# Turned tiles between the gate and the up product, and one layer norm's root on ScalarE, in a fused four-layer kernel

## The reference

```python
x = x + _layernorm(_L0_attn_ref(_layernorm(x), ...))   # state-space layer
x = x + _layernorm(_L0_ffn_ref(_layernorm(x), ...))    # 4-bit gated feed-forward
x = x + _layernorm(_L1_attn_ref(_layernorm(x), ...))   # attention over heads
x = x + _layernorm(_L1_ffn_ref(_layernorm(x), ...))    # mixture of experts
...
def _L0_ffn_ref(x, ...):
    gate = x2 @ Wg          # [1024, 512] @ [512, 1376]
    up = x2 @ Wu
    inter = gate * jax.nn.sigmoid(gate) * up
    out = (inter @ Wd).astype(jnp.float16)
...
def _layernorm(x, axis=-1, eps=1e-05):
    m = jnp.mean(x, axis=axis, keepdims=True)
    v = jnp.var(x, axis=axis, keepdims=True)
    return (x - m) / jnp.sqrt(v + eps)
```

## Time and profile before

| | |
|---|---|
| time, 3 runs | median 820.5 us (820.09 to 820.9) |
| profiled execution | 822.49 us, its span 820.6 us |
| TensorE busy | 691.6 us (84%) |
| VectorE busy | 690.7 us (84%) |
| ScalarE busy | 462.8 us (56%) |
| GpSimd busy | 488.0 us (59%) |
| granted TensorE clock, mean | 0.904 of full speed |

### The profile page before, as it was taken

The page is one execution under the profiler, slowest core; times in us unless marked ns, Lnnn a source line. Parts: engine busy times, 40 slices in busy tenths (PEclk is TensorE's granted clock), DMA queues, the critical chain, the costliest instruction groups (busy, mean ns, idle before and its releaser), DMA issues. The chain is left out here.

```text
span 820.6 us, 8369 instructions
## 1 busy us (share of the span) xinstructions
PE 691.6 (84%) x2770; PEld 326.2 (40%) x2770; DVE 690.7 (84%) x694; ACT 462.8 (56%) x783; POOL 488.0 (59%) x258
## 2 busy tenths in 40 slices
PE   7979899988685978465648879999999999999993
PEld 6623333322121323111112224444445447787882
DVE  6789899999999999999999999997364656585668
ACT  5477768777655774957554445675334447233321
POOL 2429989999999999999999920300002014340251
PEclk9999989999788998666857879999999999999997
DMA  7443122335404623633136129970040030000011
GB/s 252 95 135 103 67 101 94 125 128 198 161 4 151 208 79 139 180 128 109 46 103 215 42 78 241 244 219 5 1 153 1 1 103 0 1 1 1 0 52 51
DMA packets 42001, 82.39 MB, mean 100 GB/s; under 512 B 6743, under 2 KB 10240, under 8 KB 41704
## 3 DMA queue, kind: packets, MB, share of 16 engines
q1 hardware_dynamic: 41960, 81.87, 31.3%
HBM read 70.65 MB, written 11.21 MB: 100 GB/s over the span
## 5 line engine op out<-in xcount | busy, mean ns | idle before, releaser
L2211 POOL TENSOR_TENSOR dbu<-rep_du,bc 128x1024 f32<-128x1024 f32 x127 | 296.5, 2359 | 4.3 <-DMA rep_du<-rep_scratch 2.3
L1748 ACT ACTIVATE psum<-rep_dt,aneg 128x512 f32<-128x512 f32 x256 | 166.1, 682 | 116.7 <-DVE hc L1162 99.4
L1151 DVE TENSOR_TENSOR_SCAN psum<-psum,dbu 128x1024 f32<-128x1024 f32 x89 | 203.5, 2286 | 6.6 <-ACT psum L1748 5.0
L925 PE MATMUL psum<-hc,stk 128*32 128x512 f32 x512 | 85.4, 744 | 67.0 <-POOL hc L2220 50.0
L1162 DVE TENSOR_TENSOR hc<-psum,bc 128x1024 f32<-128x1024 f32 x89 | 109.0, 1224 | 3.1
L2220 POOL TENSOR_TENSOR hc<-hc,bc 128x1024 f32<-128x1024 f32 x39 | 91.8, 2354 | 6.0 <-DVE hc L1151 6.0
L1151 DVE TENSOR_TENSOR_SCAN hc<-psum,dbu 128x1024 f32<-128x1024 f32 x39 | 89.0, 2281 | 2.1 <-POOL dbu L2211 1.3
L680 PE MATMUL psum<-xf_hi,gu_hi 128*128 128x512 f16 x176 | 66.8, 379 | 1.3 <-DVE gu_lo L1209 0.7
L680 PE MATMUL psum<-xf_lo,gu_hi 128*128 128x512 f16 x176 | 66.7, 379 | 0.0
L680 PE MATMUL psum<-xf_hi,gu_lo 128*128 128x512 f16 x176 | 66.7, 379 | 0.0
L680 PE MATMUL psum<-xT,w_g 128*128 128x512 f32 x120 | 61.0, 658 | 2.6 <-ACT rep_du L1893 2.6
(11 more groups left out here) (268 smaller groups left out, 1450.9 us busy)
## 6 DMA issues: line engine op xcount, KB each, us to landing
rep_dt<-rep_scratch SPq DMA_DIRECT2D x60, 256.0 KB, 3.4
rep_du<-rep_scratch SPq DMA_DIRECT2D x60, 256.0 KB, 4.2
cw<-c_scratch SPq DMA_DIRECT2D x11, 768.0 KB, 10.5
qw<-qgu_in SPq DMA_DIRECT2D x11, 512.0 KB, 5.8
bc<-bc_scratch SPq DMA_DIRECT2D x16, 256.0 KB, 4.9
rep_scratch<-du_t SPq DMA_DIRECT2D x14, 256.0 KB, 2.0
rep_scratch<-dt_t SPq DMA_DIRECT2D x14, 256.0 KB, 2.3
qw<-qd_in SPq DMA_DIRECT2D x11, 256.0 KB, 7.1
```

The lines of the kernel that those rows point to most:

```text
L925: last = pe.matmul(y_rows(k), stk[:], hc[:, (i + k // 2) % HCS, k % 2, :], start=False, stop=(s == GN - 1))
L1151: dve.tensor_tensor_scan(h, a, dbu[:, i % DBS].rearrange("p e t -> p (e t)"), 0.0, ALU.mult, ALU.add)\
L1748: last = act.activation(psum[:, 2 * (i % 2) + e, :], rep_dt[:, cc % 2, k, :], ACT.Exp, scale=aneg[:, k, c, n:n + 1])
L2211: pool.tensor_tensor(dbu[:, i % DBS], rep_du[:, cc % 2, k:k + 2, :], bc[:, n, :].unsqueeze(1).broadcast_to([P, 2, L]), ALU.mult).then_inc( ...
```

## The change

1. In batch 1, at i = 4 (att) and i = 9 (moe), TensorE turns tiles 0 and 1 between g(i) and u(i), and tiles 2 and 3 between u(i) and down(i - 1); before, all four came behind down(i - 1).
2. To go with it, VectorE normalises all four tiles in the step before (i = 3 and i = 8), and takes the low halves of moe tiles 0 and 1 there too; ScalarE copies tiles 0 and 1 between the Silu and the cast of it_hi.
3. The statistics of ("out", 1) go from VectorE to ScalarE: a sum of each of four tiles between the weight casts ahead of step 0 (`sums_out`), four squares behind Silu(0), and behind Silu(1) a table load, root and shift (`own_root`). The bodies of `less_mean`, `squares` and `own_root` are those already used for batch 0's output.
4. The Silu table is asked for explicitly behind it_hi(1) and behind the roots at k = 5 and at i = 2, 6 and 8 of batch 1.

```diff
@@ -99,6 +99,7 @@
 
 
 TURN_FIRST = IC - NT
+TURN_BETWEEN = {4: "att", 9: "moe"}
 SSM_EARLY = 3
 OWN_PLACE = [item for items in SIDE.values() for item in items if item[0] == "dt"]
 ABS_AT = {2: 4, 3: 4, 7: 4}
@@ -136,13 +137,14 @@
         if i >= TURN_FIRST:
             items += [("tr", "ffn", 1, i - TURN_FIRST)]
     for i in range(IC):
-        items += [("g", 1, i), ("u", 1, i)]
-        if i == 4:
-            items += [("tr", "att", 0, t) for t in range(NT)]
+        items += [("g", 1, i)]
+        if i in TURN_BETWEEN:
+            items += [("tr", TURN_BETWEEN[i], 0, t) for t in range(2)]
+        items += [("u", 1, i)]
+        if i in TURN_BETWEEN:
+            items += [("tr", TURN_BETWEEN[i], 0, t) for t in range(2, NT)]
         if i == 5:
             items += [("qkv", 0)]
-        if i == 9:
-            items += [("tr", "moe", 0, t) for t in range(NT)]
     for b in range(NB):
         items += [("lt", b), ("routed", b, 0), ("logits", b)]
         items += [("routed", b, t) for t in range(1, NT)]
@@ -964,18 +966,15 @@
                             parts += halves(gu_hi[:, i, w], gu_lo[:, i, w], xf_hi[b][:, kk, :],
                                             xf_lo[b][:, kk, :])
                         product(item, parts).then_inc(work_ready, 1)
+                        if b == 1 and i in TURN_BETWEEN:
+                            for t in range(2 * j, 2 * j + 2):
+                                turn(TURN_BETWEEN[i], 0, t, xnc)
                     if i >= 1:
                         down(i - 1)
                     if b == 0 and i >= TURN_FIRST:
                         turn("ffn", 1, i - TURN_FIRST, obuf[1])
-                    if b == 1 and i == 4:
-                        for t in range(NT):
-                            turn("att", 0, t, xnc)
                     if b == 1 and i == 5:
                         qkv_part(0)
-                    if b == 1 and i == 9:
-                        for t in range(NT):
-                            turn("moe", 0, t, xnc)
                 down(IC - 1)
 
 
@@ -1219,8 +1218,8 @@
                     dve.tensor_tensor(xf_lo[b][:, :, cols], bank(item).rearrange("p (k t) -> p k t", k=KH),
                                       xf_hi[b][:, :, cols], ALU.subtract).then_inc(taken_sem(item), 1)
 
-            def low_moe(b):
-                for t in range(NT):
+            def low_moe(b, tiles=range(NT)):
+                for t in tiles:
                     item = ("tr", "moe", b, t)
                     cols = slice(t * P, (t + 1) * P)
                     dve.wait_ge(xmhi_done, NT * b + t + 1)
@@ -1466,18 +1465,10 @@
                     unpack(i + 3)
                 if i:
                     ffn_low(0, i)
-                if i == 1:
-                    for t in range(NT):
-                        wait_taken(dve, ("out", 1, t))
-                    stats(("out", 1), [obuf[1][:, t, :] for t in range(NT)])
                 if i == 5:
                     dve.wait_ge(out_done, NB * NT)
+                    dve.wait_ge(stats_ready, LN[("ffn", 1)])
                     stats(("ffn", 1), x_tiles(1))
-                if i == 2:
-                    inv_std(("out", 1), NT)
-                    n = LN[("out", 1)]
-                    dve.scalar_tensor_tensor(nmr1[:], mv[:, n, :, 0], -1.0, rstd[:, n, :], ALU.mult, ALU.mult)\
-                        .then_inc(nmr_ready, 1)
                 if i == 6:
                     inv_std(("ffn", 1), NT)
                     n = LN[("ffn", 1)]
@@ -1492,24 +1483,24 @@
 
             for i in range(IC):
                 ffn_times(1, i)
-                if i == 9:
-                    norm_tile("moe", 0, 2, xnc)
-                    norm_tile("moe", 0, 3, xnc)
                 ffn_low(1, i)
                 if i == 0:
                     dve.wait_ge(ld_att, 16 * 7)
                     dve.tensor_reduce(wqkv[:, :, 0:DH], wqraw[:], AX.X, ALU.add).then_inc(wq_done, 1)
                     dve.tensor_reduce(bqkv[:, 0:DH], bqraw[:], AX.X, ALU.add).then_inc(wq_done, 1)
-                if i < 8:
+                if i < 8 and i != 4:
                     between(0, i)
+                if i == 3:
+                    between(0, 4)
                 if i == 7:
                     between(0, 8)
                 if i == 8:
                     inv_std(("moe", 0), NT)
-                    norm_tile("moe", 0, 0, xnc)
-                    norm_tile("moe", 0, 1, xnc)
+                    for t in range(NT):
+                        norm_tile("moe", 0, t, xnc)
+                    low_moe(0, [0, 1])
                 if i == 9:
-                    low_moe(0)
+                    low_moe(0, [2, 3])
 
 
             def route(b):
@@ -2025,8 +2016,8 @@
                 act.copy(gu_hi[:, i, :], w[:, 0:2 * KH * P]).then_inc(whi_done, 1)
                 act.copy(d_hi[:, i, :], w[:, 2 * KH * P:]).then_inc(whi_done, 1)
 
-            def high_moe(b):
-                for t in range(NT):
+            def high_moe(b, tiles=range(NT)):
+                for t in tiles:
                     item = ("tr", "moe", b, t)
                     wait_work(act, item)
                     act.copy(xm_hi[b][:, :, t * P:(t + 1) * P], bank(item).rearrange("p (k t) -> p k t", k=KH))\
@@ -2052,6 +2043,10 @@
                     act.wait_ge(ffn_used, k - 1)
                 act.copy(it_hi[:, k % 2, :], it[:, k % 2, :]).then_inc(ithi_done, 1)
 
+            def sums_out(t):
+                wait_taken(act, ("out", 1, t))
+                link(act.activation(spare[:], obuf[1][:, t, :], ACT.Identity, accum_out=asum[:, t:t + 1]))
+
             def take16(b):
 
                 act.wait_ge(ffn_used, IC * (b + 1))
@@ -2067,14 +2062,32 @@
             whole(0)
             whole(1)
             high_weights(0)
+            sums_out(0)
+            sums_out(1)
             high_weights(1)
+            sums_out(2)
+            sums_out(3)
             whole(2)
             for k in range(NB * IC):
                 b, i = divmod(k, IC)
                 if TURN_FIRST < k < IC:
                     high_turned(1, [k - TURN_FIRST - 1])
                 ffn_silu(k)
+                if k == 0:
+                    less_mean()
+                    for t in range(NT):
+                        squares(("out", 1), t, obuf[1][:, t, :])
+                if k == 1:
+                    act.preload_act_table_set(LOG_EXP)
+                    own_root(("out", 1), nmr1, nmr_ready)
+                if b == 1 and i == 4:
+                    take_turned("att", 0, 0, xTa[0])
+                    take_turned("att", 0, 1, xTa[0])
+                if b == 1 and i == 9:
+                    high_moe(0, [0, 1])
                 ffn_high(k)
+                if k == 1:
+                    act.preload_act_table_set(SILU)
                 if k + 2 < IC:
                     high_weights(k + 2)
                 if k + 3 < IC:
@@ -2083,17 +2096,15 @@
                     high_turned(1, [NT - 1])
                     take16(0)
                 if b == 1 and i == 4:
-                    for t in range(NT):
-                        take_turned("att", 0, t, xTa[0])
-                if k == 1:
-                    act.preload_act_table_set(LOG_EXP)
-                    root(("out", 1), NT)
+                    take_turned("att", 0, 2, xTa[0])
+                    take_turned("att", 0, 3, xTa[0])
                 if k in (2, 3):
                     for t in range(2 * k - 4, 2 * k - 2):
                         norm_out(1, t)
                 if k == 5:
                     act.preload_act_table_set(LOG_EXP)
                     root(("ffn", 1), NT)
+                    act.preload_act_table_set(SILU)
                 if k in (TURN_FIRST - 1, TURN_FIRST):
                     first = 2 * (k - TURN_FIRST + 1)
                     for t in range(first, first + 2):
@@ -2117,8 +2128,10 @@
                     if i in (3, 4):
                         high_moe_chunk(0, 1, "wr", 2 * (i - 3))
                         high_moe_chunk(0, 1, "wr", 2 * (i - 3) + 1)
+                    if i in (2, 6, 8):
+                        act.preload_act_table_set(SILU)
                     if i == 9:
-                        high_moe(0)
+                        high_moe(0, [2, 3])
                         high_moe_chunk(1, 2, "up", 0)
                     if i == 10:
                         for n in range(1, KH):
```

## The result

The changed kernel takes 829.85 us (median of 4 runs, 828.65 to 830.89); before it was 820.46 us (4 runs). The ratio is 1.0104, 95% interval 1.0090 to 1.0119: it is slower by 1.0%, some 9 us. The forecast was 829.5 us.

What follows compares the result with a forecast made beforehand. In the gated feed-forward TensorE, working in written order, was taken as the pace. 3.3 + 2.3 - 0.4 + 3.8 = +9.0 us took the median from 820.5 to 829.5 us; 8-in-10 range 824.0 to 832.5.

Steps and rivals of the forecast that it cites:

- The place of the turns: Batch 1: TensorE waits 3.6 us at i = 4 and 3.4 at i = 9 for tiles; costs +3.3 and +2.3 us.
- The clock: Behind the waits at i = 4 and i = 9 TensorE's clock halves: 2.3 and 1.5, +3.8 us; ends 0 and 6.0.
- Batch 0: Statistics moved to ScalarE: down(0) 0.4 us late, g(3) near 513.9 instead of 514.32; -0.4 us, from -0.9 to +1.2.
- The wait for gu_hi: Batch 0: second table load puts gu_hi(3) at 512.5; VectorE's 3 us of statistics become a wait for ScalarE.
- Edits at nothing: Explicit Silu loads, ScalarE's tiles ahead of it_hi(4) and it_hi(9), and a semaphore wait cost nothing; no load moves.
- From the profiled execution to the median: Whole kernel: sum made on the profiled 822.5 us, giving 831.5, then put on the median 820.5, 2.0 below.
- The clock stays: Rival at i = 4 and i = 9: both waits come without a clock fall; +5.2, 825.7 us, chance 0.14.
- The drain behind a table load: Rival in batch 0: about 1380 ns drain per load, +2.7 us on ScalarE before g(3); 832.2 us, chance 0.02.

Runs made afterwards that it cites:

- the fillers: Changed kernel plus fourteen products nobody reads ahead of the first turn at i = 4 and i = 9; 826.05 us, ratio 1.0067 against the kernel before.
- the att run: Kernel before with only the att tiles 0 and 1 turned between g(4) and u(4), statistics on VectorE; 825.76 us, ratio 1.0051.
- the late root: Kernel before with ScalarE statistics, turns as before, table load, root and shift behind step 1, no Silu load behind it_hi(1); 821.36 us, ratio 1.0001.
- both places: Changed kernel's turns at i = 4 and i = 9 alone, statistics, root and shift of ("out", 1) as before; 828.96 us, ratio 1.0090.
- moe: Kernel before with only the moe tiles 0 and 1 turned between g(9) and u(9), statistics on VectorE; 825.23 us, ratio 1.0043.
- statistics alone: Changed kernel with the turns put back as before, keeping ScalarE statistics, root, shift and explicit Silu tables; 820.99 us, ratio 0.9994.
- w_wr later: Changed kernel with the four casts of w_wr moved one step on, to i = 4 and 5; 828.22 us, ratio 1.0089.

## Why the prediction was right

**The place of the turns.** The step was that TensorE reaches tiles 0 and 1 about 3.5 us before they are normalised, and that all work behind them is ready and waits. The trace has 3.68 and 3.40 us for the forecast 3.6 and 3.4. With the clock kept by the fillers i = 4 costs 3.1 us (forecast 3.3) and i = 9 costs 2.2 (2.3). The runs with one place each show the two add up.

**The clock.** It fell at both places, as forecast. The price was 3.8 us, 2.3 and 1.5; the trace has 2.2 and 1.0, and the fillers gave back 3.0 to 3.8. Over the three profiled executions of each place the terms are 1.6 and 1.8 in the mean, so the sum was a little high, and the reason for making the second the smaller, its shorter hole, is not borne out.

**Batch 0.** The forecast -0.4 us cannot be told from nothing in the timed run (-0.06%, give or take 0.12), and the -0.65 of the trace comes with a g(0) that was 1.0 us early; it also lies outside the 0.5 us that the prediction named for g(3). So this term is open: it is small, and its sign is not shown. The sizes inside it were off. down(0) waits 1.03 us for it_lo(0), not 0.4: g(0) itself started 1.0 us earlier in this execution, where TensorE had the clock at 1.00 from 488 to 494. The execution of before had 0.88, the second row, columns as in the earlier trace rows:

```profile
488.00:494.00 6.00, 6.00 (x21) 2.58 (x20) 5.97 (x8) 2.31 (x6) 0.00 (x0) 1.00 0.58 190
488.00:494.00 6.00, 6.00 (x16) 2.43 (x15) 5.79 (x7) 0.41 (x2) 0.00 (x0) 0.88 0.46 152
```

The wait for gu_hi came as worked out.

**Edits at nothing.** The load at 612.30 still stands right behind its root, and no second load was saved or added. That held.

**From the profiled execution to the median.** Here a step was incomplete. I carried the difference of 2.0 us between the profiled execution of before and its median over as it was. The fall of the clock from 715 to 718, which one execution has and the next has not, is worth 1.5 us and may be most of it; the timed executions have no traces that would show it. After, the profiled execution lies 1.2 us below its median. The forecast of the median, made by adding to the median, was not hurt by it.

**What of the agreement is luck.** 829.5 was forecast and 829.85 measured. The four executions of the changed kernel spread over 2.2 us, and the change is 8.5 us by the ratio and 9.4 by the medians. The terms as the traces have them are 5.3 us for the waits, 3.4 for the clock in the mean, and between -0.65 and 0 for batch 0: 8.0 to 8.7, against 9.0. The mechanism held; that the median was met to 0.4 us is luck.

**The rivals.** "The clock stays" is what the fillers make by hand, at 826.05 us for the 825.7 worked out for it. The drain behind a table load showed nowhere: in the changed kernel the next instruction starts 0.01 to 0.02 us behind each load, where it does not wait for another engine.

## What to carry to other kernels

An engine that works strictly in order and is the pace should meet an item of another chain only when that item is ready. Before moving one forward, compare the time at which its last input is written with the time at which the engine would reach it; here the same move, with two tiles left where they were and two one place later, won some 3 us where the change lost 9. The two waits cost 5.3 us by themselves and some 3 us more by the clock that fell behind them, and filling them with products that nobody reads gave that part back. And moving work off a busy engine wins only if its queue does not then wait for the engine that got the work: three orders of the same root could not be told apart.

## What the runs showed of the hardware

- The clock fell while TensorE was busy all the time: in the execution of before, and in those of the att run, of the fillers and of the late root, it stood at 0.5 for some 3 us directly behind the attention's qkv product of batch 1, whose matmuls are 128x48. The execution of the att run shows it, columns as in the earlier trace rows:

```profile
717.00:721.00 4.00, 4.00 (x35) 3.84 (x34) 1.10 (x1) 0.57 (x1) 1.15 (x1) 1.00 0.00 0
721.00:725.00 4.00, 4.00 (x14) 3.21 (x14) 3.48 (x4) 0.00 (x0) 0.00 (x0) 0.57 0.00 0
725.00:729.00 4.00, 4.00 (x19) 3.30 (x18) 1.32 (x2) 2.02 (x3) 2.29 (x2) 1.00 0.00 0
```

  The other nine profiled executions, that of the changed kernel among them, kept it at 1.00 there. It is worth 1.5 us: from g(10) to the end the four that lost it take 151.2 to 151.3 us, and the changed kernel, both places, moe, statistics alone and w_wr later 149.6 to 149.7. This is one cause of what the timed executions of one kernel differ by, up to 4.6 us for the att run, and not the only one.
- What the clock costs behind one and the same wait is not one number: behind a wait of 3.4 us at i = 9 it was 1.0, 1.7 and 2.6 us in three executions.
- VectorE's normalisation of a 128x512 fp32 tile takes 0.54 us alone and 1.5 us while GpSimd subtracts 128x512 tiles. The Trainium skill, GPSIMD Engine Reference, section Key points, states that GpSimd and VectorE share their way to SBUF and contend where VectorE works in a 2-port mode or with two SBUF inputs. The rows agree that there is contention; in which mode VectorE was they don't show.
